# Wide attention scores as three float32r products, and softmax sums turned by one transpose and spread by DMA

## The reference

```
xn = layernorm(x)
norm_q  = rmsnorm(xn @ W_cq)  * q_scale          # 128 wide
norm_kv = rmsnorm(xn @ W_ckv) * kv_scale         # 64 wide
q = [norm_q @ W_dq_nope, rope(norm_q @ W_dq_rope)]   # 16 heads, 128 + 64
k = [norm_kv @ W_dk_nope, rope(xn @ W_krope) / 16]   # rope part is shared
scores = q k^T / sqrt(192), causal;  attn = softmax(scores)
out = (attn @ (norm_kv @ W_dv)) @ W_o
ffn = sum over the top 6 of 32 experts (silu(xn wg) * (xn wu)) wd, plus a shared expert
result = x + out + ffn
```

## Time and profile before

| | |
|---|---|
| median of 3 runs | 1383.71 us |
| the profiled execution | 1379.22 us |
| its span | 1377.3 us |
| TensorE busy | 1286.7 us, 93% |
| VectorE busy | 842.3 us, 61% |
| ScalarE busy | 858.1 us, 62% |
| GpSimd busy | 616.4 us, 45% |
| scores, first and last stage (L1126, L1561) | 169.7 and 169.8 us |
| ten transposes a head (L1148, L1583) | 80.4 and 80.3 us |

### The profile page before, as it was taken

One profiled execution on the slowest core, in us unless ns is written; L12 is line 12 of the kernel. 1 busy time (PEld: TensorE's weight loads), 2 busy tenths in 40 slices (PEclk: granted clock), 3 DMA queues, 4 the chain that ended last, 5 costly groups with the idle time before them and its releaser, 6 DMA issues. The chain is left out here.

```text
span 1377.3 us, 24088 instructions
## 1 busy us (share of the span) xinstructions
PE 1286.7 (93%) x7385; PEld 957.9 (70%) x7385; DVE 842.3 (61%) x2695; ACT 858.1 (62%) x2326; POOL 616.4 (45%) x542
## 2 busy tenths in 40 slices
PE   4999759999999999969999999997999999999997
PEld 3666436767777677758788888886667766777765
DVE  4577678777787687723333333333777777777774
ACT  1455427776677577635556666664777777777673
POOL 1111118777775777720000000001888888887820
PEclk8999979999999999999999999998999999999999
DMA  9977663233326432259966666664655665765510
GB/s 343 404 271 276 245 235 120 100 105 112 112 101 254 159 101 88 90 157 328 334 218 195 184 186 186 193 184 125 104 88 90 128 100 87 132 106 89 98 26 31
DMA packets 147281, 223.24 MB, mean 162 GB/s; under 512 B 13847, under 2 KB 128215, under 8 KB 142295
## 3 DMA queue, kind: packets, MB, share of 16 engines
q1 hardware_dynamic: 99350, 157.72, 33.8%
q0 software_dynamic: 36864, 53.50, 18.7%
q10 hardware_dynamic: 10944, 10.49, 2.5%
HBM read 105.27 MB, written 116.39 MB: 161 GB/s over the span
## 5 line engine op out<-in xcount | busy, mean ns | idle before, releaser
L1519 POOL DMA_INDIRECT l_sums<-sorted_y,slot_no x192 | 299.3, 1559 | 421.6 <-DMA l_sums<-base_dram 363.4
L1067 POOL DMA_INDIRECT sorted_x<-f_xn_row,slot_no x192 | 204.8, 1067 | 49.3 <-issue 44.8
L1223 ACT ACTIVATE f_prob<-f_prob,f_negmax 128x512 f32<-128x512 f32 (+3 forms) x256 | 142.6, 558 | 121.1 <-DVE f_negmax L1294 119.9
L2069 DVE SCALAR_TENSOR_TENSOR act_f<-hidden,rows_in,ps 128x96 f32<-128x96 f32 x224 | 70.4, 314 | 229.8 <-ACT hidden L2032 229.6
L1672 ACT ACTIVATE l_prob<-l_prob,l_negmax 128x512 f32<-128x512 f32 (+3 forms) x256 | 141.6, 555 | 104.0 <-DVE l_negmax L1754 102.9
L1994 PE MATMUL ps<-wgu_sb,xt_e 128*128 x896 | 184.6, 329 | 0.5 <-issue 0.3
L1561 PE MATMUL ps<-l_kt,l_qt 128*128 128x512 f32 (+3 forms) x512 | 169.8, 446 | 5.3 <-DVE l_qt L1747 4.8
L1126 PE MATMUL ps<-kt_s,f_qt 128*128 128x512 f32 (+3 forms) x512 | 169.7, 446 | 4.9 <-DVE f_qt L1287 4.3
L1294 DVE CUSTOM_DVE_ANT_0 f_prob<-ps,mask_add 128x512 f32<-128x512 f32 (+3 forms) x256 | 120.6, 486 | 86.2 <-PE ps L1126 85.4
L1754 DVE CUSTOM_DVE_ANT_0 l_prob<-ps,mask_add 128x512 f32<-128x512 f32 (+3 forms) x256 | 120.6, 486 | 83.3 <-PE ps L1561 82.1
L1994 PEld LDWEIGHTS ps<-wgu_sb,xt_e 128*128 128x128 f32 x896 | 140.7, 191 | 2.7 <-issue 2.1
(11 more groups left out here) (192 smaller groups left out, 2623.0 us busy)
## 6 DMA issues: line engine op xcount, KB each, us to landing
sorted_x<-zeros SPq DMA_DIRECT2D x14, 2304.0 KB, 10.1
rows_in<-sorted_x SPq DMA_DIRECT2D x112, 288.0 KB, 3.1
sorted_y<-rows_out SPq DMA_DIRECT2D x112, 256.0 KB, 2.1
wgu_sb<-in_wgu SPq DMA_DIRECT2D x16, 384.0 KB, 5.7
x_in<-in_x SPq DMA_DIRECT2D x8, 512.0 KB, 10.4
xn_dram<-xn SPq DMA_DIRECT2D x8, 512.0 KB, 4.1
base_dram<-x_in SPq DMA_DIRECT2D x8, 512.0 KB, 3.0
nqt_dram<-nqt_out SPq DMA_DIRECT2D x8, 512.0 KB, 3.9
```

The costliest lines, as they stand in the source:

```text
L1067: pool.indirect_dma_start(sorted_x, bass.IndirectOffsetOnAxis(ap=slot_no[:, t, k:k + 1], axis=0), xn_row[buf][:], None).then_inc(scattered ...
L1223: act.activation(prob[:, i, qt, 0:w], prob[:, i, qt, 0:w], ACT.Exp, bias=negmax[:, i, qt:qt + 1], scale=-1.0, accum_out=rowsum[:, g // 2 % ...
L1519: pool.indirect_dma_start(sums[n % NSUM][:, t, :], None, sorted_y, bass.IndirectOffsetOnAxis(ap=slot_no[:, TT * GROUPS[n] + t, k:k + 1], a ...
```

## The change

- `Q_ORDER` becomes `[1, 3, 2, 0]`: 256, 512, 384, 128 keys. Scores of the tiles 2 and 3 (384 and 512 keys) are three float32r products; the other two stay float32.
- For that ScalarE makes the high part of each head's queries for these tiles (`queries_hi`, 128x256) and of each batch's keys (`keys_hi`, 128x512), VectorE the low part of the queries (`queries_lo`), GpSimd that of the keys (`keys_lo`).
- The sums [128, 8] of a pair are turned by one transpose to [8, 128] at `g = 2p + 2`, after the ten transposes (`turn_sums`). VectorE takes the reciprocal of [8, 128] out of PSUM, now between its third and fourth maximum. SyncE stores it to `norms_dram`, waits, and loads it back in two DMAs that repeat each row in 64 partitions. The spread, the four transposes and `copy_norms` go.
- The shuffle of the rope (`queries_swap`) moves to the end of the even head, `queries_sum` of the first head ahead of the third maximum.
- SyncE's program follows the heads: `during` is dissolved into `step`, the kept weights go in 16 stores of 256 KB, one for each pair of batches 1 and 2, the first experts' weights one part a pair in batch 3.
- The zero rows are half as long (`ZCOLS` 1152), so that the fills of `sorted_x` have pieces of half the size.

```
-Q_ORDER = [3, 2, 1, 0]
+Q_ORDER = [1, 3, 2, 0]
+FIRST_SPLIT = 2
...
+            def spread_inverses(b, p):
+                sp.wait_ge(rinv_ready, NP_ * b + p + 1)
+                sp.dma_start(norms_dram[p % 2], inverse[:, p % 2, :]).then_inc(norms_stored, 16)
+                sp.wait_ge(norms_stored, 16 * (NP_ * b + p + 1))
+                sp.wait_ge(lat_normed, NP_ * b + p)
+                for i in range(2):
+                    sp.dma_start(norms[i * KVR:(i + 1) * KVR, :].rearrange("r (t q) -> r t q", t=TT),
+                                 norms_dram[p % 2, i * TT:(i + 1) * TT, :].unsqueeze(0).to_broadcast([KVR, TT, P]))\
+                        .then_inc(norms_loaded, 16)
+            def keep(n):
+                k, at = n // (2 * QUART), n % QUART
+                part = slice(2 * at, 2 * at + 2)
+                if n // QUART % 2 == 0:
+                    sp.dma_start(wq_dram[k][:, part], wq_s[k][:, part].bitcast(F32)).then_inc(kept, 16)
+                else:
+                    sp.dma_start(wvo_dram[k][:, part], wvo_s[k][:, part].bitcast(F32)).then_inc(kept, 16)
+            def step(bt, g):
+                b, p = bt.now, g // 2
+                if g % 2 == 0 and bt.back(g, 2):
+                    spread_inverses(bt.back(g, 2)[0], bt.back(g, 2)[1] // 2)
...
+                if g % 2 == 1 and g < NH:
+                    if b in (1, 2):
+                        keep(NP_ * (b - 1) + p)
...
             def scores(b, g, k):
+                if k == 1:
+                    pe.wait_ge(q_lo, NH * b + g + 1)
+                    if g == 0:
+                        pe.wait_ge(k_lo, b + 1)
...
+                if n >= FIRST_SPLIT:
+                    rows = slice((n - FIRST_SPLIT) * P, (n - FIRST_SPLIT + 1) * P)
+                    mm = product3(pe, s_ps[k % 2][:, 0:w], [q[g % 2][:, rows] for q in q_s],
+                                  [part[b % 2][:, 0:w] for part in k_s], True, True)
+                else:
+                    mm = pe.matmul(s_ps[k % 2][:, 0:w], qt[g // 2 % 2][g % 2][:, n * P:w], kt_s[:, b, 0:w], start=True, stop=True)
...
-            def turn_norms(b, p):
+            def turn_sums(b, p):
                 pe.wait_ge(q_abs, min(NH * b + 2 * p + 6, NH * HB))
+                pe.wait_ge(exp_done, unit(b, 2 * p + 2))
+                pe.transpose(sums_ps, rowsum[:, p % 2].rearrange("p i t -> p (i t)"), ident[:]).then_inc(sums_turned, 1)
...
+            def queries_hi(b, h):
+                act.wait_ge(q_turned, NH * b + h + 1)
+                act.wait_ge(q_abs, NH * b + h + 1)
+                act.activation(q_s[0][h % 2][:], qt[h // 2 % 2][h % 2][:, FIRST_SPLIT * P:S], ACT.Copy).then_inc(q_hi, 1)
...
+            def queries_lo(b, h):
+                dve.wait_ge(q_hi, NH * b + h + 1)
+                dve.tensor_tensor(q_s[1][h % 2][:], qt[h // 2 % 2][h % 2][:, FIRST_SPLIT * P:S],
+                                  q_s[0][h % 2][:].bitcast(F32), ALU.subtract).then_inc(q_lo, 1)
...
             def inverses(b, p):
+                if NP_ * b + p > 1:
+                    dve.wait_ge(norms_stored, 16 * (NP_ * b + p - 1))
+                dve.wait_ge(sums_turned, NP_ * b + p + 1)
+                dve.reciprocal(inverse[:, p % 2, :], sums_ps).then_inc(rinv_ready, 1)
```

More of the change, by code:

```diff
@@ L929, in heads_first @@
     qt = [[room_b.sb(f"f_qt{i}{j}", [P, S]) for j in range(2)] for i in range(2)]
+    q_s = [[sb(f"f_q_{part}{i}", [P, S - FIRST_SPLIT * P], F32R) for i in range(2)] for part in ("hi", "lo")]
+    k_s = [[sb(f"f_k_{part}{i}", [P, S], F32R) for i in range(2)] for part in ("hi", "lo")]
     negmax = sb("f_negmax", [P, 2, TT])
     rowsum = sb("f_rowsum", [P, 2, 2, TT])
-    rinv = sb("f_rinv", [P, 2, 2, TT])
-    spread = sb("f_spread", [P, 2, TT, 2, KVR])
+    inverse = sb("f_inverse", [2 * TT, 2, P])
     one = sb("f_one", [P, 1])
@@ L1201, in step @@
                     turn(*bt.back(g, 1))
+                if par == 0 and bt.back(g, 2):
+                    b, h = bt.back(g, 2)
+                    turn_sums(b, h // 2)
                 if g < NH:
@@ L1252, in step @@
                     exps(bt.now, g, 0)
+                if g < NH and par == 0:
+                    queries_hi(bt.now, g + 1)
                 if nxt and par == 0:
@@ L1357, in step @@
                 if nxt and par == 1:
-                    queries_sum(*nxt, 0)
+                    queries_lo(nxt[0], 2 * nxt[1])
+                if now and par == 0:
+                    queries_lo(bt.now, g + 1)
                 if par == 1 and bt.back(g, 1):
                     turned(*bt.back(g, 1))
+                if par == 0 and bt.back(g, 2):
+                    b, h = bt.back(g, 2)
+                    inverses(b, h // 2)
                 if now:
@@ L1393, in heads_last @@
     qt = [[room.sb(f"l_qt{i}{j}", [P, S]) for j in range(2)] for i in range(2)]
+    q_s = [[sb(f"l_q_{part}{i}", [P, S - FIRST_SPLIT * P], F32R) for i in range(2)] for part in ("hi", "lo")]
+    k_s = [[sb(f"l_k_{part}{i}", [P, S], F32R) for i in range(2)] for part in ("hi", "lo")]
     negmax = sb("l_negmax", [P, 2, TT])
     rowsum = sb("l_rowsum", [P, 2, 2, TT])
-    rinv = sb("l_rinv", [P, 2, 2, TT])
-    spread = sb("l_spread", [P, 2, TT, 2, KVR])
+    inverse = sb("l_inverse", [2 * TT, 2, P])
     prob = room.sb("l_prob", [P, 2, TT, S])
```

277 lines of the change are left out of this document (159 added, 118 removed).

## The result

The changed kernel takes 1391.26 us (median of 6 runs, 1388.84 to 1393.5), the kernel before 1384.07 (6 runs, 1381.52 to 1386.39). The ratio is 1.0052, 95% interval 1.0037 to 1.0068: slower by 7.2 us, where 3.7 less was forecast. The profiled execution took 1393.5 us with a span of 1390.8. The traces say in which stretches the 13.5 arose, the experiments how much of it is real.

The account below looks back on a forecast made before the run. TensorE bounds, busy 98.51 of 100 us. Profiled 1379.2 - 5.4 (pairs) - 4.2 (weight stores) + 3.8 (tails) + 2 (keys' high copy) = 1375.4 us, so a median of 1380, interval 1352 to 1406.

Parts of the forecast that it names:

- TensorE's work of 9.92 us a pair: Per pair of heads, 10.84 us less 0.92 saved by float32r scores and dropped transposes.
- the stall: TensorE waits 0.89 us a pair before the odd head's 512-key score, for the 128-key maximum behind the reciprocal.
- the pair without a piece of 10.81 us: Pair of heads without output piece: 9.92 us of work plus 0.89 waiting; both stages together save 5.4 us.
- the broadcast: Inverses stored to DRAM and loaded back in 6.1 us, bounds 5.1 and 8.2, hidden by 1 us before the latents.
- the weight stores: Four 1 MB stores no longer issued together, removing TensorE's idle time and lower clock there: -4.2 us, bounds 0 and -6.
- rival A: The inverse is hidden, costing near its lower bound of 0.10 us: 38 us less, 1342 us; chance 0.12.
- (3): Keys' high copy in ScalarE's queue delays the values, +2 us; GpSimd's low part of the keys has ample time.
- B: The broadcast comes late at VectorE's latent multiply: +32 us, 1412 us; chance 0.14.
- C: VectorE and ScalarE tighten further, slack before the inverse gone: 0.25 us a pair, +16, 1396 us; chance 0.23.
- (2): Tails of both stages: last sums wait for two DMAs in a row, +2.8 us in the last, +1 in the first.
- (4): Half as long zero rows and startup splits: 0 us, between -2 and +3.
- Rival D: Float32r products run slower than the query products: 0.1 us a product, +0.6 a pair, 1418 us; chance 0.03.

Follow-up runs that it names:

- run 6: Changed kernel with all scores as plain float32 products again, the high and low parts still made: 1421.54 us, 1.0274 to the kernel before.
- run 5: Changed kernel with the reciprocal taken of the 128x8 sums before the small transpose, a copy in its old place: 1357.56 us, 0.9797 to the kernel before.
- run 1: Changed kernel with the keys' low part in the first heads formed by VectorE instead of GpSimd: 1383.77 us, 0.9992 to the kernel before.
- Run 9: Changed kernel with keys' low part on VectorE and early inverse; tails with inverses spread by products 1349.21 us, with busy TensorE 1346.86, with both 1344.18.
- run 8: Kernel before with only the zeros' tile 1152 wide instead of 2304 and the output tile's new place: 1387.21 us, 1.0023.

## Why the prediction was wrong

**Right, with its sizes.** TensorE's work of 9.92 us a pair (10.86 less the stall of 0.88 is 9.98; its plain scores back cost 11.44 - 10.86 = 0.58 by run 6, for 0.50), the reciprocal of 0.95 us for 8x128, the pair without a piece of 10.81 us (10.84 to 10.88), the place, size and releaser of the stall, the broadcast hidden but for five short waits, the weight stores (-4.4 for -4.2), VectorE at 84.65 for 88. The same 0.95 us put at the 0.10 us of rival A would by its working give 38 us; run 5 gave 34.

**The step that failed** is in (3) of what else moves: "GpSimd's low part of the keys has eight heads of time." I asked only whether it comes in time, and it does. It costs by running at all: it holds VectorE's two-operand instructions, and with VectorE at work for 10.4 of 10.86 us most of a hold reaches TensorE (1.7 to 2.1 us of idle time for a product lengthened by 2.2 to 2.6), twice with the clock's fall behind it. Costed at nothing, it measured 9.7 us in the traces and 8 by run 1. Without it the change would have been 0.9992, no difference, 3 to 4 us above my forecast. None of my rivals was this mechanism: B and C put the loss into every pair, and the pairs without a piece lost nothing. The length of such a hold was on record: GpSimd's subtraction of 128x512 was already there once a pair before, at 1.27 us, and met nothing.

**Mis-sized.** (2) The tails were forecast at 3.8 us and took 7.8. Up to the last latents they lost 1.4 and 3.4 us, for 1 and 2.8: the DMAs were nearly right. The other 2.9 us lie behind the latents, where the clock is lower after TensorE's longer idle time; my walk had a chain at full speed. Run 9 shows that a busy TensorE keeps the clock. (4) The start, put at 0 with +3 as its end, took 4.2 us in the trace and about 3 by run 8. The ScalarE part of (3), put at 2 us, cost nothing while the pair was 10.86 us long. The pairs gave 3.8 us for 5.4: in the first heads the first of the two pieces of a round has a pair of 14.05 us where it had 13.70, in the last heads one of 14.47 where it had 14.68. These two errors nearly cancel, which is luck.

**Slips in the sums.** Rival D has 12 split products a pair, so 0.1 us each is 1.2 a pair and not 0.6. The upper bound of the broadcast, 8.2 us, is 7.9 from its own terms. Neither touched the forecast.

**Argued, not shown.** The cause of the 14.05 us was not separated; GpSimd's low part of the latents, which holds VectorE for 0.5 us in every such pair, is a candidate. That the weights' spread alone is worth 4.4 us rests on the trace, no run undid it. Why four pieces a partition are late and three are not, stays open.

## What to carry to other kernels

Ask of an instruction that GpSimd is to run not only whether it comes in time but which of VectorE's instructions it meets, and where both of that one's operands are in SBUF, count GpSimd's full length against the engine that waits for VectorE. When two engines close a loop of nearly equal length, shorten the work in it; moving it gained nothing here. Take a reciprocal in the layout with the fewest elements per lane, and turn the result.

## What the hardware showed

- A reciprocal costs 0.95 us for 8x128 and for 128x128, and 0.20 for 128x8: it goes by the elements in a lane, however few lanes work.
- A VectorE subtraction of two SBUF tiles, 0.42 us alone, took 1.98 us on average where it met a GpSimd product of 1.87 us (0.63 over all), and 0.42 where it met a GpSimd fill of 1.12 us.
- GpSimd's subtraction, 1.27 us alone, took 1.74 where VectorE's sum of two SBUF tiles had started just before it: the hold goes both ways.
- TensorE's idle 1.71 us in the first heads left the clock at 1.00; idle 2.00 and 2.14 us brought it down, to 0.65 (358 to 362 us) and 0.73 (461 to 465 us).
- In the last tail an idle 1.57 + 0.46 us left TensorE at clock 1.00, and 1.68 + 1.08 us brought values of 4.07 instead of 2.38 us. With products that nothing reads in the gaps the clock stayed at 1.00.
- Fills from zeros in pieces of 4.6 KB put the first score at 195.4 to 198.1 us; with pieces of 6.1 and 9.2 KB it came at 193.64 and 193.65.
